# Attentions: the rank matmuls one step later, the third expert's raw weights fetched five steps earlier, fixed PSUM pairs for four steps

## What is computed

```python
x = x + xattn0(layernorm(x), ctx)   # 16 heads of 16, softmax(QK/4 - 0.1*|i-j|) V, output projection
x = x + ffn0(layernorm(x))          # dense silu MLP 256-1024-256, plus product-key experts:
                                    # top 8 of 64 x 2 keys per head, 4 heads, 8 of 1024 experts
x = x + xattn1(layernorm(x), ctx)   # relu(Wq), relu(Wk), relu(Wv), softmax(QK/4) V
x = x + ffn1(x)                     # layernorm -> softmax gate over 8 experts, top 2;
                                    # out = sum over the 2 of  w * W2 gelu(W1 x)
```

## Time and profile before

| | us |
|---|---|
| runs, median (lowest to highest) | 1135.71 (1132.48 to 1136.11) |
| the profiled execution, by the clock of the runs | 1129.27 |
| its span, first to last instruction | 1127.5 |
| PE busy | 1001.2 (89% of the span) |
| DVE busy | 783.4 (69%) |
| ACT busy | 652.5 (58%) |
| POOL busy | 497.7 (44%) |
| mean granted clock of TensorE, share of full speed | 0.955 |

### The profile page before, as it was taken

How to read it: one execution, slowest core, us unless ns; L and a number is a source line. 1 busy time by engine, 2 the same in 40 slices (tenths; PEclk the granted TensorE clock), 3 DMA queues, 4 the chain that set the end, 5 groups by cost and what they waited for, 6 DMA issues and landing times.

```text
span 1127.5 us, 17009 instructions
## 1 busy us (share of the span) xinstructions
PE 1001.2 (89%) x5550; PEld 633.1 (56%) x5550; DVE 783.4 (69%) x1755; ACT 652.5 (58%) x874; POOL 497.7 (44%) x550
## 2 busy tenths in 40 slices
PE   8789999989778989989999779899998887999991
PEld 3345444434466778778777564344443333888881
DVE  7767688887888787787787346788888845344443
ACT  3356667666566766676677434576675560555550
POOL 6458898896415434433543342115051435122220
PEclk9899999999999999999999999999999889999996
DMA  8754979648999600000002231376554328222226
GB/s 245 224 171 161 289 194 354 192 156 267 230 220 217 124 1 1 1 2 0 1 6 74 62 104 54 112 209 150 149 148 121 96 81 342 62 70 71 71 62 224
DMA packets 74201, 149.89 MB, mean 133 GB/s; under 512 B 7823, under 2 KB 44577, under 8 KB 72580
## 3 DMA queue, kind: packets, MB, share of 16 engines
q1 hardware_dynamic: 61380, 98.80, 34.0%
q0 software_dynamic: 10800, 47.63, 11.9%
q10 hardware_dynamic: 1936, 2.36, 0.6%
HBM read 73.14 MB, written 76.25 MB: 133 GB/s over the span
## 4 chain that ended last, share of the span: by engine, by line
PE 63%; DVE 14%; ACT 10%; issue 5%; DMA 3%; POOL 3%; SPq 1%; ACTq 0%; DVEq 0%; POOLq 0%
PE ps L1313 15%; PE ps L1447 10%; PE ps L1428 7%; PE ps L1413 5%; PE ps L1387 4%; PE ps L1397 3%; PE ps L1655 3%; ACT pt L1105 3%; PE ps L1618 3%; PE ps L1632 3%; DVE negmax L1852 2%; PE ps L1776 2%; PE ps L1456 2%; PE ps L1331 1%; DVE moe_w L2198 1%
## 5 line engine op out<-in xcount | busy, mean ns | idle before, releaser
L1852 DVE TENSOR_REDUCE negmax<-ps 128x2 f32<-128x1024 f32 x256 | 309.7, 1222 | 60.2 <-PE ps L1413 58.2
L1105 ACT ACTIVATE pt<-ps 128x1024 f32<-128x1024 f32 x256 | 259.2, 1027 | 137.4 <-PE ps L1428 135.6
L1447 PE MATMUL ps<-pt,v_aug 128*32 128x512 f32 x1024 | 145.4, 634 | 3.9 <-POOL pt L804 3.1
L1428 PE MATMUL ps<-sq,sk 57*128 57x512 f32 (+1 forms) x512 | 129.2, 503 | 6.8 <-DMA sq<-m_sb 3.9
L1413 PE MATMUL ps<-sk,sq 56*128 56x512 f32 (+1 forms) x512 | 108.5, 429 | 18.8 <-ACT pt L1105 15.0
L804 POOL TENSOR_TENSOR pt<-pt,near 128x256 f32<-128x256 f32 x128 | 92.5, 730 | 51.0 <-ACT pt L1105 50.4
L1428 PEld LDWEIGHTS ps<-sq,sk 57*128 57x128 f32 (+1 forms) x512 | 49.4, 190 | 109.1 <-issue 71.0
L996 POOL DMA_INDIRECT expert_out<-yo,dest x39 | 38.1, 977 | 116.4 <-ACT yo L1280 101.7
L908 POOL TENSOR_TENSOR w_first<-w_first,moe_w 128x1024 f32<-128x1024 f32 x16 | 38.1, 2380 | 104.4 <-DVE pt L2190 103.6
L1618 PE MATMUL ps<-sel,hl 128*128 128x512 f32 x256 | 72.3, 415 | 5.1 <-DVE pt L2190 5.1
L1413 PEld LDWEIGHTS ps<-sk,sq 56*128 56x128 f32 (+1 forms) x512 | 50.5, 194 | 40.5 <-ACT pt L1105 28.4
(11 more groups left out here) (323 smaller groups left out, 2059.5 us busy)
## 6 DMA issues: line engine op xcount, KB each, us to landing
expert_rows<-zero SPq DMA_DIRECT2D x3, 5586.0 KB, 61.7
expert_weights_split<-wst POOLq DMA_DIRECT2D x8, 2048.0 KB, 8.5
qk_rows<-hl SPq DMA_DIRECT2D x30, 512.0 KB, 3.1
sk<-qk_rows SPq DMA_DIRECT2D x62, 192.0 KB, 5.0
sq<-qk_rows SPq DMA_DIRECT2D x62, 192.0 KB, 4.5
moe_w<-in_w POOLq DMA_DIRECT2D x16, 512.0 KB, 7.7
wexp<-expert_weights_split POOLq DMA_DIRECT2D x16, 512.0 KB, 4.8
wexp<-expert_weights_split SPq DMA_DIRECT2D x4, 2048.0 KB, 16.7
```

The source lines that it names most:

```text
L1105: act.activation(pt[:, 4 * (U % 2) + 2 * half:4 * (U % 2) + 2 * half + 2, :], ps[:, bank:bank + 2, :], ACT.Exp, scale=(BIAS, SCALE)[L]).th ...
L1428: ins = pe.matmul(ps[:, key.bank + s, :], sk[r, pair, c * P:(c + 1) * P], sq[r, pair, :], start=True, stop=True)
L1447: ins = pe.matmul(ps[32 * j:32 * j + 32, OBANK, :], v_aug[:, b % 2, c, HG * g + j, :], pt[:, 4 * (U % 2) + j, :], start=(c == 0), stop=(c ...
L1852: dve.tensor_reduce(negmax[:, n % 2, col:col + 9:8], ps[:, job.bank:job.bank + 2, :], AX, ALU.max, negate=True).then_inc(s_jd, 1)
```

## The change

Three edits, all in what the planner and POOL's loop read.

1. `ROUTE`: rk in step 32 instead of 31 of its batch, for batches 0 to 2 (steps 32, 48 and 64 of the second attention). The last batch keeps its steps.
2. `LOAD_RAW`: the raw weights of expert 2 are fetched in step 10 instead of 15.
3. In the first attention the scores by key of steps 60 to 63 take the fixed pairs (2,3) for half 0 and (4,5) for half 1, nt 1 takes bank 0 and nx 1 bank 1. `next_pair()` isn't called for them, so whoever asks next gets the pair that key 60 had.

```diff
+LATE = 60
+LATE_BANKS = {("nt", 1): 0, ("nx", 1): 1}
...
-ROUTE = whole({23: ("gt", 0), 24: ("gt", 1), 25: ("gl", 0), 31: ("rk", 0)})
+ROUTE = whole({23: ("gt", 0), 24: ("gt", 1), 25: ("gl", 0), 32: ("rk", 0)})
...
-LOAD_RAW = (15, 16, 22, 28, 34, 40)
+LOAD_RAW = (10, 16, 22, 28, 34, 40)
...
             elif kind == "s":
                 banks = next_pair()
+            elif (kind, i) in LATE_BANKS:
+                banks = (LATE_BANKS[kind, i],)
...
         def add_keys(U, half):
-            banks = next_pair()
+            banks = next_pair() if L or U < LATE else (2 + 2 * half, 3 + 2 * half)
```

## The result

| | before | after |
|---|---|---|
| median of the runs | 1135.91 us (1132.48 to 1137.04) | 1122.48 us (1119.96 to 1124.53) |
| profiled execution, its span | 1129.27, 1127.5 us | 1123.61, 1121.8 us |
| mean granted clock | 0.955 | 0.957 |

The ratio is 0.9886, with an interval of 0.9863 to 0.9909; the medians lie 13.4 us apart. The profiles differ by only 5.7 us of span. That difference is the first thing to explain, and part of the experiments is for it.

What follows compares the result with a forecast made beforehand. PE, busy 1001.2 of 1127.5 us, was taken to bound the kernel. Edit 2's -3.7, edit 1's -8.0 and edit 3's +1.6 sum to -10.1 us, from 1135.7 to 1125.6 us, range 1119.0 to 1132.5.

Steps and rivals of the forecast that it cites:

- the 10.1 of the sum: Whole kernel: gains of 3.7 and 8.0 us less a loss of 1.6, from 1135.7 to 1125.6 us.
- Edit 2, forecast 3.7: First attention, steps 17 to 20: POOL's 5.31 us wait for expert 2's weights goes, gaining 3.7 us, bounds 0 and 4.5.
- the cover behind the wait: Step 20's maxima were covered by POOL's stall; without it a delay of up to 1 us may show.
- a sign of being wrong: Edit 2 counts as wrong if the wait reappears at step 20 on the maxima SP sends in step 18.
- Edit 1, forecast 8.0 = 2.2 + 3.5 + 2.3: Second attention: later ranks remove PE's waits for picked experts in the first, second and third batch; bounds 3 and 9.5.
- the low clock behind the gap: Second batch's ranks: two of four steps, 17.64 us in all, ran at lower clock; without the gap 13.2.
- DVE's floor: Second batch's four steps: DVE has 13.12 us of work, so about 14.1 us is the floor, 3.5 gained.
- has its own sends done before: Third batch: POOL starts its last rows at 942.54 behind the ranks' chain, its own sends already done.
- Edit 3, forecast a loss of 1.6: End of first attention: nt 1's gap goes, but step 63's keys wait for ot 3.2's emptying; gain 4.0 to loss 8.
- The offset to the median: Profiled execution was 6.4 us below the runs' median; the same difference was put on the forecast median.
- The bank edit pays in full: Rival, end of first attention: fixed pairs gain 4.0 instead of losing 1.6, DVE not waited for; 1120.0 us, chance 0.15.
- The slow case: Ot 3.2's wait holds the low clock through logits and hidden products, 8 us lost; 1140.7 us, chance 0.06.

Runs made afterwards that it cites:

- s2_after: The changed kernel run again without further edits, compared with the kernel before: 1121.55 us, ratio 0.9864 (0.9817 to 0.9911).
- s3_best: The changed kernel with expert 2's load at step 12, ot 3.2 in bank 0 and the last batch's norm moved from POOL to ACT: 1122.35 us, 0.9915.
- s1_before: The kernel before run again, unchanged, as a null comparison: 1134.35 us, ratio 1.0022 (0.9996 to 1.0048).
- s1_load: The kernel before with only expert 2's raw weights fetched in step 10 instead of 15: 1130.26 us, ratio 1.0005 (0.9976 to 1.0034).
- s1_banks: The kernel before with only the fixed pairs in steps 60 to 63 of the first attention: 1130.22 us, ratio 1.0005 (0.9978 to 1.0033).
- s3_noranks: The changed kernel with the ranks of batches 0 to 2 back at step 31: 1131.20 us, 1.0004, beside 1123.44 us for the changed kernel.
- s1_ranks: The kernel before with only the ranks of batches 0 to 2 moved to step 32: 1123.3 us, ratio 0.9945 (0.9927 to 0.9964).

## Why the prediction was right, and where it wasn't

The forecast was 1125.6 us in a range of 1119.0 to 1132.5. The first comparison gave 1122.48 us, and all executions together gave 9.5 us of gain against the 10.1 of the sum. The ranks carry the gain, as forecast; the early load brought less than forecast, the fixed pairs lost about what was forecast, and that the total fits so well is partly luck. By its own steps:

- **Edit 2, forecast 3.7.** The wait went, and steps 18 to 20 became 3.7 us shorter in the first pair of profiles (A19-20, 7.61 to 3.91). The means of the ledger are 7.2 with step 15 and 4.5 with step 10, so 2.7. What failed is the cover behind the wait: of the 4.0 us lost the sum keeps 3.7, and so leaves 0.3 for late maxima and late stacks together. The prediction calls a wait on the maxima in step 20 a sign of being wrong, and it is there in every profile with the load moved, 0.45 to 1.38 us long. The stacks came late as well: steps 13 and 14 became longer in six of the seven profiles with step 10, by 0.2 to 5.8 us, 1.5 on the mean of the seven. Net about 1.2, not 3.7. The bounds (0 to 4.5) hold on the mean, but not for s2_after, which lost 3 us. The Trainium skill's rule that transfers of two issuing engines interleave (DMA: Bandwidth & Descriptors, section Issuing engines are not separate DMA queues) weighed more than I gave it: the traces agree with it by those 1.5 us.
- **Edit 1, forecast 8.0 = 2.2 + 3.5 + 2.3.** First batch 2.3, in every pair, with DVE the next limit as said. Second batch: 4.3 in the first pair, but 1.0 against three of the five kernels without the edit. The step that failed is costing the low clock behind the gap as if it always came. DVE's floor was put too high as well: 14.1 us for a stretch that took 13.35 at 94% DVE, near the 13.2 worked out without DVE. Third batch: PE's last values end at 919.48 instead of 925.45, of which 3.6 was won earlier, so 2.4 us. The sentence that POOL "has its own sends done before" was wrong: in both kernels its norm stands right behind batch 2's sends, which end 0.04 us ahead of it. In before the rows came 2.93 us behind the norm and it cost nothing; in the changed kernel the norm is what the sends wait for, and the last sends win 942.54 - 936.38 = 6.16 us, not the 8.2 by which the last ranks came earlier on PE (931.28 against 939.50). But s3_best shows that POOL hid DVE by 1.2 us only. From the last mark of the ledger (B63) to the end all nine kernels with the edit are at 206.3 to 207.0, the five without at 208.9 to 211.6, 3.3 us on the means. In sum 2.3 + 1.0 to 4.3 + 3.3 = 6.6 to 9.9; measured alone 6.2 (4.1 to 8.3), and 7.8 when taken back out of the changed kernel.
- **Edit 3, forecast a loss of 1.6.** The mechanism is shown: PE waits 4.49 us for DVE's emptying of ot 3.2 (4.49 or 4.50 in all six kernels with the fixed pairs alone), until 289.98 (forecast 291.1, for a kernel that wasn't yet 1.1 us ahead), and bank 0 for it takes the wait away. In the first pair of profiles the changed kernel is 1.08 us ahead at step 61 and starts the second attention 0.52 us behind, a loss of 1.6. On the means from A61 to B0 it is 1.8, inside the spread, and by time, alone or taken back, it wasn't measurable. The Trainium skill's advice to rotate independent groups through the banks (Perfetto Trace Analysis, section Matmuls) agrees in sign with this loss. It isn't the pinning that costs, though: with a bank of its own for ot 3.2 the stretch isn't longer than with rotation (396.1 against 397.4 on the means of three and five profiles, a difference inside the spread). One reading behind the 1.6 was wrong: the last values of the kernel before, 1.98 us in the earlier trace rows, did not run at the low clock. Their window (length, busy, clock, DMA share, GB/s) is at full clock; four of the eight matmuls waited for POOL's second near bias.

```profile
292.45:294.43 1.98, 1.98 (x9) 1.00 1.11 219
```

  In the changed kernel the clock in the same place is down to 0.50. So the clock was no ground for a small loss, and that 1.6 us came out all the same is luck in that part.
- **The offset to the median.** I set after's median 8.2 us above the span of its forecast, as before's was. After's lies 0.7 us above its span. Before's first profile was simply one of its quick executions: s1_before lies where the runs are. So this term was 7.5 us too large, and the span came out 4.4 us above its forecast (1121.8 against 1117.4). The two cancel in part, and that is why the forecast's error against the first comparison is only 3.1 us. That is luck.
- **The rivals.** "The bank edit pays in full" came nearest in time (1120.0) and is wrong as a mechanism; fixed pairs pay only with ot 3.2 moved as well. DVE is the next bound behind the ranks, but took back little. The slow case didn't come: in the changed kernel the clock is 0.50 from 289 to 295 us, 0.89 in the two us from 295 on, where the logits start (295.50), and 1.00 behind.

What remains open is why the changed kernel's executions are so even (1119.8 to 1127.5) and before's are not. s1_load, s1_banks and s3_noranks reach up to 1142.8, 1136.2 and 1137.3 us, s1_ranks only to 1127.2. So the waits for the picked experts are part of it, and the ledger shows one way, the clock behind the second of them; the 7 us in B35-47 of s1_before came ahead of that wait and aren't explained by it. Nor does a run show why before's executions are mostly long on chip 2 (eight of nine at 1134 to 1140 us and a clock of 0.941 to 0.948) and mixed on chip 13.

## What to carry to other kernels

Read a stretch in several executions before costing it: what looks like the price of a gap may be a low clock that came in two of five profiles. Here the gap of 1.36 us ahead of the second batch's ranks was worth 1.0 us every time, and the low clock behind it 2.2 or 3.3 more sometimes. When a transfer is issued earlier, list what the other issuing engines send in the same microseconds and issue behind them: in the profiles two steps later avoided the late stacks and kept the gain. When buffers are pinned, look at who else still takes from the rotation: the one user left in it brought a wait of 4.5 us, and a bank of its own for it took 4.1 us off the time. Compare on the same chip, and more than once.

## What the runs showed of the hardware

- TensorE's clock fell with no gap ahead of it. In the changed kernel PE was busy 4.00 of 4.00 us before the fall, and no row waited (PE windows: length, busy, clock, DMA share, GB/s):

```profile
843.00:847.00 4.00, 4.00 (x32) 1.00 0.67 117
847.00:851.00 4.00, 4.00 (x21) 0.67 0.29 111
851.00:855.00 4.00, 3.68 (x16) 0.50 0.01 2
```

The profile of before held 1.00 there with the same work; all thirteen others fall to 0.50 somewhere from 842 to 857 us. B35-47 took 41.83 us in it and 43.3 to 49.0 in the other thirteen: the forecast's base had a piece of luck of 2.4 us in one place, against the median of the others.

- The timeline of ACT calls the end of that 2.20 us stand in s1_before remote. Five other profiles (s1_load, s1_banks, s1_ranks, s3_noranks, s3_best) have such a row about 2 us on, of 0.87 to 0.90 us, and another of 0.41 behind it, and eight have none in the second attention. It belongs to no edit, and what it is no run here shows.
